# An LSTM's input term: added by TensorE from a ring of bfloat16 parts, or laid into PSUM by ScalarE

## The chip, the core and the metric

The kernel runs on one core of a Trainium2 chip. The metric is the device time of one execution in microseconds (us). Five engines work from queues of their own: TensorE (PE in the profile; PEld is its loading of weights), VectorE (DVE), ScalarE (ACT), GpSimd (POOL) and SyncE (SP), which only issues transfers here. They are ordered by semaphores alone: an instruction waits until a counter has reached a value and raises another when it is done. Before an engine stands a sequencer that reads the queue, does the register arithmetic and hands instructions on; its own instructions have the engine's name with a q in the profile (ACTq, DVEq).

## What is computed

The input x has 2 batches of 1024 time steps with 256 features. A first layer scales x by a conditioning vector, multiplies it by a weight, normalises it and adds it to x. The second layer, in which nearly all the time goes, is an LSTM over the 1024 steps, whose output is added to its input:

```python
xW = jnp.einsum('ntd,dk->tnk', x, Wx) + b
def step(carry, xw_t):
    prev_h, prev_c = carry
    a = xw_t + prev_h @ Wh
    i = jax.nn.sigmoid(a[:, :Hdim])
    f = jax.nn.sigmoid(a[:, Hdim:2 * Hdim])
    o = jax.nn.sigmoid(a[:, 2 * Hdim:3 * Hdim])
    g = jnp.tanh(a[:, 3 * Hdim:])
    next_c = f * prev_c + i * g
    next_h = o * jnp.tanh(next_c)
    return ((next_h, next_c), next_h)
```

Hdim is 256, so a step has 1024 gate values for each of the 2 batches, and each step needs the h of the one before.

## The kernel before

**Layout.** A feature lies on a partition: the 256 values of h are K = 2 chunks of 128 partitions, each with B = 2 batches, thus CB = 4 columns. The 1024 gate values are M = 8 chunks (two for each of the gates i, f, o, g), thus ITEMS = 16 columns of a step. x*Wx+b lies in the tile `xw` with the step as the fastest index (`xw[:, item, time in a block of 128]`). Only the first 17 items (chunk and batch of a block of 128 steps) are computed ahead of the loop (line 668); the loop computes one more in each of its turns and so keeps a block ahead.

**The loop** has 128 turns of 8 steps, written out; each engine has its own copy of it. In a step:

- TensorE (lines 505 to 559) does 12 matmuls that bring x*Wx+b into the gates' PSUM banks: `ring` holds it as three bfloat16 parts for 8 steps, and each part is multiplied by a bfloat16 identity (`input_apart`, `input_together`). They wait for `f_act`, `c_done` and `o_act`, that is, until ScalarE and VectorE have read what the last step left in the bank. In steps 2 to 7 of a turn it also does two of the 12 matmuls that project the item for a later block (`project`, 128 columns, bank X_BANK). Then it waits for `h_hi` and does 44 matmuls of Wh with h, both as two float16 parts, which accumulate onto the input: 8 for gate i with the high part of h, 8 for f (these wait for `h_lo`), 8 for g, 8 for i with the low part, 4 for half of o, 8 for the rest. After f, g, i and o they raise `f_mm`, `g_mm`, `ig_in`, `o0_mm` and `o_in`. All matmuls are recorded at line 389, the helper.
- VectorE (lines 697 to 726) sums the two halves of f (line 703) and of g (705), multiplies the cell state by sigmoid(f) (707), sums o (709), does the cell update as a scan (712), then the high part of h (715, raises `h_hi`), the low part (718, raises `h_lo`) and h itself for the output (722, raises `h_all`). In step 4 of a turn it also transposes the turn's output (726).
- ScalarE (lines 777 to 798) does the sigmoid of f (785), of i and g (788) and of o (790), and the tanh of the cell (792). In the last step of a turn it moves the projected item from PSUM into `xw` (797): it waits for `x_mm`, raises `act_seen` by a semaphore instruction, works out the addresses in registers, and does one ACTIVATE of 128 columns.
- GpSimd (lines 343 to 378) splits the next turn's x*Wx+b into three bfloat16 parts, four operations for each half of a turn (lines 287, 292, 297, 302), splits 8 steps of x in the same way (366 to 373), and adds the layer's input to h (308). Each group waits for a step's `h_all`.
- SyncE (from line 237) copies the weights and the piece of x for the next projection and stores the output.

**Ahead of the loop** VectorE works out scales (lines 629 to 646), which ScalarE needs to scale and split the weights (762 to 766, then GpSimd 319 and 322); TensorE projects the first 17 items and the first layer.

Of the kernel before, what the change touches and what calls it, by code (L numbers as in the profile page):

```python
# [27 lines left out]
P = 128  # L28
# [18 lines left out]
def cond_resid_lstm(nc, x, cond, w, wx, wh, bias, out):  # L47
# [13 lines left out]
    with ExitStack() as ctx:  # L61
# [13 lines left out]
        ident_b = sb("ident_b", [P, P], BF16)  # L75
# [15 lines left out]
        x_unit = sb("x_unit", [P, 1])  # L91
        w_scale = sb("w_scale", [P, 1])
# [3 lines left out]
        xw = sb("xw", [P, NI, P])  # L96
# [10 lines left out]
        ring = sb("ring", [P, UNROLL, G, 3, CB], BF16)  # L107
        rest = sb("rest", [P, M * B, HALF])
# [24 lines left out]
        pre_ig = psum[:, I_BANK:G_BANK + 1, sums]  # L133
        cell = banks[CELL][:, 0:3 * CB].rearrange("p (c s) -> p c s", s=3)
# [6 lines left out]
        s_zero, s_ident, s_identb, s_ones = sem("s_zero"), sem("s_ident"), sem("s_identb"), sem("s_ones")  # L141
# [12 lines left out]
        ring_full, ring_used = sem("ring_full"), sem("ring_used")  # L154
# [96 lines left out]
        def _(pool):  # L251
# [5 lines left out]
            pool.wait_ge(s_ident, 1)  # L257
            nc.gpsimd.tensor_copy(ident_b[:, :], ident[:, :]).then_inc(s_identb, 1)

            def xw_of_step(t0):

                block, inside = t0 // P, t0 % P
                if not isinstance(t0, int):
                    block, inside = pool.snap(block * ITEMS), pool.snap(inside)
                else:
                    block = block * ITEMS
                return xw[:, bass.ds(block, ITEMS), bass.ds(inside, HALF)]

            def parts(half, part):  # L270
                return ring[:, half * HALF:(half + 1) * HALF, :, part, :].rearrange("p s g c -> p g c s")

            def by_gate(ap):
                return ap.rearrange("p (g c) s -> p g c s", g=G)
# [5 lines left out]

            def xw_source(half, turn):

                return by_gate(xw_of_step(turn * UNROLL + half * HALF if isinstance(turn, int) else pool.snap(turn * UNROLL + half * HALF)))

            def split_high(half, src):

                nc.gpsimd.tensor_copy(parts(half, 0), src).then_inc(s_pool, 1)  # L287
                settle()

            def split_rest(half, src):  # L290

                nc.gpsimd.tensor_tensor(by_gate(rest[:, :, :]), src, parts(half, 0), ALU.subtract).then_inc(s_pool, 1)
                settle()

            def split_middle(half):

                nc.gpsimd.tensor_copy(parts(half, 1), by_gate(rest[:, :, :])).then_inc(s_pool, 1)  # L297
                settle()

            def split_low(half):  # L300

                nc.gpsimd.tensor_tensor(parts(half, 2), by_gate(rest[:, :, :]), parts(half, 1), ALU.subtract).then_inc(ring_full, 1)  # L302
# [21 lines left out]
            for s, v in last_read("xw"):  # L324
                pool.wait_ge(s, v)
            pool.wait_ge(s_start, 1)
            for half in range(2):
                src = xw_source(half, 0)
                split_high(half, src)
                split_rest(half, src)  # L330
                split_middle(half)
                split_low(half)
# [4 lines left out]
            def calm_after(step):  # L337

                pool.wait_ge(h_all, step)
                pool.sem_inc(pool_seen, 1)  # L340

            with pool.Fori(0, NI - 1) as i:
# [4 lines left out]
                pool.wait_ge(x_read, i + 1)  # L347
                pool.sem_inc(pool_seen, 1)
                for half in range(2):
                    done = t + (half + 1) * HALF  # L350
                    src = xw_source(half, i + 1)
                    pool.wait_ge(ring_used, 1)
                    pool.sem_inc(ring_used, -1)
                    calm_after(done)
                    split_high(half, src)
                    split_rest(half, src)
                    calm_after(done + 1)
                    if half == 0:
                        pool.wait_ge(y_turned, i + 1)
                        pool.sem_inc(pool_seen, 1)  # L360
                    save(half, t + half * HALF)
                    split_middle(half)
                    calm_after(done + 2)
                    split_low(half)
                    if half == 0:
                        nc.gpsimd.tensor_copy(part[0], now).then_inc(s_pool, 1)
                        settle()
                        calm_after(done + 3)
                        nc.gpsimd.tensor_tensor(res, now, part[0], ALU.subtract).then_inc(s_pool, 1)
                        settle()  # L370
                        nc.gpsimd.tensor_copy(part[1], res).then_inc(s_pool, 1)
                        settle()
                        nc.gpsimd.tensor_tensor(part[2], res, part[1], ALU.subtract).then_inc(x_split, 1)
# [7 lines left out]
        def _(pe):  # L381
# [98 lines left out]
            def in_ring(gate, u, part, first, last):  # L480
                return ring[:, u, gate, part, B * first:B * last].rearrange("p (c b) -> p c b", b=B)
# [343 lines left out]
```

## Time and profile of the kernel before

| | |
|---|---|
| median of 3 runs | 2023.9 us (2023.67 to 2024.75) |
| the profiled execution | 2023.3 us, of which its span (first to last instruction) is 2021.5 us |
| loop | 1024 steps, about 1.93 us each |
| busy share of the span | PE 98%, PEld 88%, DVE 63%, ACT 36%, POOL 30% |
| granted TensorE clock, mean | 0.51 of full speed |

A busy PE is not a PE at its peak: the matmuls are pipelined, and each is shown with its whole way through the array, 166 ns, while one starts about every 27 ns. The share therefore says little here; what waits for what in a step says more.

### The profile page before, as it was taken

What the parts mean: (1) busy time and instruction counts of PE and PEld (TensorE: products, weight loads), DVE (VectorE), ACT (ScalarE), POOL (GpSimd) and SP (SyncE); (2) the same over time, 40 slices, a digit from 0 to 9 for tenths busy, and PEclk for the clock granted to TensorE, in tenths of its full rate; (3) what the DMA queues carried; (4) which work ended last, traced back from release to release, by engine and by line L of the source; (5) the groups of instructions that cost most, each with busy time, mean ns of one, the idle gap of its engine ahead of it and who ended that gap; (6) DMA issues with size and microseconds to landing.
All of it is one profiled execution on the core that took longest, in us unless ns stands there. A gap on an engine that the chain in (4) does not pass through costs nothing.

```text
span 2021.5 us, 148186 instructions
## 1 busy us (share of the span) xinstructions
PE 1991.1 (98%) x59057; PEld 1770.8 (88%) x59057; DVE 1266.6 (63%) x8393; ACT 736.6 (36%) x4239; POOL 601.7 (30%) x1800
## 2 busy tenths in 40 slices
PE   8999999999999999999999999999999999999998
PEld 6888888888888888888888888888888888888887
DVE  6666666666666666666666666666666666666665
ACT  3333333333333333333333333333333333333333
POOL 2323233223323232332323233232323332332322
PEclk9555555555555555555555555555555555555555
DMA  2111111111111111111111111111111111111010
GB/s 96 21 21 27 20 21 26 21 20 21 27 20 21 23 24 20 21 27 20 20 21 26 20 21 27 21 20 21 27 20 21 23 24 20 21 27 20 21 22 20
DMA packets 188304, 48.63 MB, mean 24 GB/s; under 512 B 185468, under 2 KB 187784, under 8 KB 188296
## 3 DMA queue, kind: packets, MB, share of 16 engines
q1 hardware_dynamic: 188024, 48.26, 11.5%
q10 hardware_dynamic: 272, 0.26, 0.0%
q8 instruction: 5, 0.08, 0.0%
q14 instruction: 3, 0.02, 0.0%
HBM read 4.46 MB, written 2.10 MB: 3 GB/s over the span
## 4 chain that ended last, share of the span: by engine, by line
PE 95%; DVE 2%; ACT 1%; issue 1%; DMA 1%; SPq 0%; POOL 0%; POOLq 0%; DVEq 0%
PE psum L389 95%; DVE psum L712 1%; ACT scan_in L788 1%; DMA wx_sb<-in_L_cond_Wx_dram 1%; DVE psum L705 0%; DVE wmax L626 0%; SPq L203 0%; POOL wx_sb L315 0%; DVE xt L605 0%; SPq L205 0%; SPq L198 0%; SPq L199 0%; POOLq L61 0%; PE psum L435 0%; POOL y_cols L308 0%
## 5 line engine op out<-in xcount | busy, mean ns | idle before, releaser
L389 PE MATMUL psum<-h_parts,wh_p 128*128 128x2 f16 (+1 forms) x45056 | 1368.9, 166 | 0.0
L389 PEld LDWEIGHTS psum<-h_parts,wh_p 128*128 128x128 f16 x45056 | 1284.9, 104 | 46.8
L389 PE MATMUL psum<-ring,ident_b 128*128 128x4 bf16 (+2 forms) x12288 | 635.1, 168 | 19.1 <-DVE psum L680 2.6
L389 PEld LDWEIGHTS psum<-ring,ident_b 128*128 128x128 bf16 x12288 | 487.8, 105 | 185.0 <-DVE psum L712 165.0
L785 ACT ACTIVATE sig_f<-psum 128x4 f32<-128x4 f32 x1024 | 177.7, 174 | 1034.9 <-DVE psum L703 1034.9
L703 DVE TENSOR_REDUCE psum<-psum 128x4 f32<-128x8 f32 x1024 | 178.5, 174 | 389.0 <-PE psum L389 389.0
L389 PE MATMUL psum<-x_piece,wx_piece 128*128 128x128 bf16 x1536 | 411.0, 268 | 0.0
L715 DVE SCALAR_TENSOR_TENSOR h_parts<-scan_h 128x4 f16<-128x4 f32 x1024 | 174.2, 170 | 246.8 <-ACT scan_h L792 246.8
L287 POOL CAST ring<-xw 128x64 bf16 (+1 forms) x256 | 120.9, 472 | 601.0 <-DVE hring L722 600.8
L790 ACT ACTIVATE scan_h<-psum 128x4 f32<-128x4 f32 x1024 | 179.2, 175 | 142.3
L718 DVE TENSOR_TENSOR_SCAN h_parts<-scan_h,h_parts 128x12 f16<-128x12 f32 x1024 | 187.0, 183 | 35.0
L302 POOL TENSOR_TENSOR ring<-rest,ring 128x64 bf16<-128x64 f32 x256 | 124.8, 488 | 282.2 <-DVE hring L722 281.8
L705 DVE TENSOR_REDUCE psum<-psum 128x4 f32<-128x8 f32 x1024 | 178.5, 174 | 39.9
L788 ACT ACTIVATE scan_in<-psum 128x8 f32<-128x8 f32 x1024 | 185.4, 181 | 44.7
L712 DVE TENSOR_TENSOR_SCAN psum<-scan_in 128x12 f32<-128x12 f32 x1024 | 195.8, 191 | 0.0
L707 DVE TENSOR_TENSOR scan_in<-sig_f,psum 128x4 f32<-128x4 f32 x1024 | 164.3, 160 | 27.2
L792 ACT ACTIVATE scan_h<-psum 128x4 f32<-128x4 f32 x1024 | 179.8, 176 | 0.0
L709 DVE TENSOR_REDUCE psum<-psum 128x2 f32<-128x4 f32 x1024 | 174.4, 170 | 0.0
L389 PEld LDWEIGHTS psum<-x_piece,wx_piece 128*128 128x128 f16 x1536 | 159.8, 104 | 0.0
L722 DVE TENSOR_TENSOR hring<-scan_h 128x4 f32<-128x4 f32 x1024 | 153.6, 150 | 0.0
L297 POOL CAST ring<-rest 128x64 bf16<-128x64 f32 x256 | 120.7, 471 | 0.3 <-POOLq L279 0.3
L308 POOL TENSOR_TENSOR y_cols<-xt,hring 128x16 f32<-128x16 f32 x256 | 58.5, 229 | 208.5 <-DVE y_rows L726 115.7
(93 smaller groups left out, 410.4 us busy)
## 6 DMA issues: line engine op xcount, KB each, us to landing
x_piece<-x_p SPq DMA_DIRECT2D x128, 192.0 KB, 2.7
wx_piece<-wx_p SPq DMA_DIRECT2D x128, 128.0 KB, 2.4
out_dram<-y_rows SPq DMA_DIRECT2D x512, 4.0 KB
x_rows<-in_x_dram SPq DMA_DIRECT2D x4, 512.0 KB, 6.4
wh_sb<-in_L_cond_Wh_dram SPq DMA_DIRECT2D x1, 1024.0 KB, 9.7
wx_sb<-in_L_cond_Wx_dram SPq DMA_DIRECT2D x1, 1024.0 KB, 11.5
w_sb<-in_L_cond_weight_dram ACTq DMA_DIRECT2D x1, 256.0 KB, 2.8
small_rows<-in_cond_dram SPq DMA_DIRECT2D x1, 2.0 KB
```

The costliest lines, as they stand in the source:

```text
L389: return nc.tensor.matmul(out_, lhs, rhs, start=first, stop=last, skip_group_check=True)
L703: nc.vector.tensor_reduce(by_chunk(pre_f), parts_of(GATE_F, K), AX.X, ALU.add).then_inc(f_sum, 1)
L705: nc.vector.tensor_reduce(by_chunk(pre_g), parts_of(GATE_G, K), AX.X, ALU.add).then_inc(ig_in, 1)
L707: nc.vector.tensor_tensor(scan_b[:, :, 2], sig_f[:, :], cell[:, :, 2], ALU.mult).then_inc(cell_in, 1)
L709: nc.vector.tensor_reduce(by_chunk(pre_o0), parts_of(GATE_O, 1), AX.X, ALU.add).then_inc(o_in, 1)
L712: nc.vector.tensor_tensor_scan(flat(cell), flat(scan_a), flat(scan_b), 0.0, ALU.mult, ALU.add).then_inc(c_done, 1)
L715: nc.vector.scalar_tensor_tensor(out=h_parts[:, 0, :, 2], in0=scan_h[:, :, 1], scalar=2.0 ** H_SCALE, in1=scan_h[:, :, 2], op0=ALU.mult, o ...
L718: nc.vector.tensor_tensor_scan(flat(h_parts[:, 1, :, :]), flat(scan_h[:, :, :]), flat(h_parts[:, 0, :, :]), 0.0, ALU.mult, ALU.subtract).t ...
L785: nc.scalar.activation(sig_f[:, :], pre_f, ACT.Sigmoid, scale=unscale).then_inc(f_act, 1)
L788: nc.scalar.activation(sig_ig, pre_ig, ACT.Sigmoid, scale=unscale).then_inc(cell_in, 1)
L790: nc.scalar.activation(scan_h[:, :, 1].rearrange("p (h b) -> p h b", b=B), pre_o, ACT.Sigmoid, scale=unscale).then_inc(o_act, 1)
L792: nc.scalar.activation(scan_h[:, :, 2], cell[:, :, 2], ACT.Tanh).then_inc(t_done, 1)
```

## The change

ScalarE lays x*Wx+b of the next step into the gates' banks with five ACTIVATEs (function Copy) from `xw`, whose layout is turned so that the 16 columns of one step lie side by side. Where two columns of a bank are summed later (f, g and half of o), half of the value goes into each (`share` is 1 or 0.5). `h_hi` now counts three events a step: the copies of f and i, and the high part of h. The copies of g and o have semaphores of their own, for which TensorE waits in the midst of its 44 matmuls. `ring`, the bfloat16 split on GpSimd, the identity matmuls and their waits go.

```diff
-        xw = sb("xw", [P, NI, P])
+        xw = sb("xw", [P, T + UNROLL, ITEMS])
...
-        ring = sb("ring", [P, UNROLL, G, 3, CB], BF16)
-        rest = sb("rest", [P, M * B, HALF])
+        units = sb("units", [P, M])
```

GpSimd, in the loop (`after_step` is the old `calm_after`; the waits on `x_read`, `ring_used` and the four splitting operations of each half are gone):

```diff
+                after_step(t + 1)
+                nc.gpsimd.tensor_copy(part[0], now).then_inc(s_pool, 1)
+                settle()
+                after_step(t + 2)
+                nc.gpsimd.tensor_tensor(res, now, part[0], ALU.subtract).then_inc(s_pool, 1)
+                settle()
+                after_step(t + 3)
+                nc.gpsimd.tensor_copy(part[1], res).then_inc(s_pool, 1)
+                settle()
+                after_step(t + HALF)
+                pool.wait_ge(y_turned, i + 1)
                 pool.sem_inc(pool_seen, 1)
...
+                save(0, t)
+                after_step(t + HALF + 1)
+                nc.gpsimd.tensor_tensor(part[2], res, part[1], ALU.subtract).then_inc(x_split, 1)
+                after_step(t + UNROLL)
+                save(1, t + HALF)
```

TensorE:

```diff
                 for u in range(UNROLL):
-                    if u % HALF == 0:
-                        pe.wait_ge(ring_full, 2 * i + u // HALF + 1)
                     if u == FIRST_PIECE:
                         pe.wait_ge(x_staged, 32 * i + 32)
                         pe.wait_ge(x_read, i + 1)
-                    pe.wait_ge(f_act, t + u + 1)
-                    input_apart(GATE_F, u, 0, K)
                     if u >= FIRST_PIECE:
                         project(done)
                         done += 1
-                    pe.wait_ge(c_done, t + u + 1)
-                    input_apart(GATE_G, u, 0, K)
-                    input_together(GATE_I, I_BANK, u, 0, K)
-                    pe.wait_ge(o_act, t + u + 1)
-                    input_apart(GATE_O, u, 0, 1)
-                    last = input_together(GATE_O, O_REST, u, 1, K)
-                    if u % HALF == HALF - 1:
-                        last.then_inc(ring_used, 1)
                     if u >= FIRST_PIECE:
                         last = project(done)
                         done += 1
                         if done == len(terms):
                             last.then_inc(x_mm, 1)
-                    pe.wait_ge(h_hi, t + u + 1)
+                    pe.wait_ge(h_hi, (t + u + 1) * 3)
                     products(GATE_I, I_BANK, 0, 0, K)
                     pe.wait_ge(h_lo, t + u + 1)
                     products_apart(GATE_F, 0, K).then_inc(f_mm, 1)
+                    pe.wait_ge(g_add, t + u + 1)
                     products_apart(GATE_G, 0, K).then_inc(g_mm, 1)
                     products(GATE_I, I_BANK, 1, 0, K).then_inc(ig_in, 1)
+                    pe.wait_ge(o_add, t + u + 1)
                     products_apart(GATE_O, 0, 1).then_inc(o0_mm, 1)
```

VectorE, ahead of the loop and in it:

```diff
+            link(nc.vector.memset(share[:, :], 1.0))
+            nc.vector.memset(share[:, GATE_F * K:GATE_F * K + K + 1], 0.5)
+            link(nc.vector.memset(share[:, GATE_G * K:M], 0.5))
...
-            nc.vector.tensor_scalar(bias_s[:, :], small[:, B * K:NSMALL], scales[:, 0:1], None, ALU.mult).then_inc(s_bias, 1)
-            nc.vector.tensor_tensor(x_unit[:, :], scales[:, 0:1], scales[:, 3:4], ALU.mult).then_inc(s_bias, 1)
+            nc.vector.scalar_tensor_tensor(out=bias_s[:, :], in0=small[:, B * K:NSMALL], scalar=scales[:, 0:1], in1=share[:, :],
+                                           op0=ALU.mult, op1=ALU.mult).then_inc(s_bias, 1)
+            nc.vector.tensor_scalar(top[:, :], share[:, :], scales[:, 0:1], None, ALU.mult).then_inc(s_bias, 1)
+            link(nc.vector.tensor_tensor(x_unit[:, :], scales[:, 0:1], scales[:, 3:4], ALU.mult))
+            nc.vector.tensor_scalar(units[:, :], share[:, :], x_unit[:, :], None, ALU.mult).then_inc(s_bias, 1)
...
+            nc.vector.memset(xw[:, T:T + UNROLL, :], 0.0)
...
-                nc.vector.tensor_scalar(xw[:, v, :], bank[:, 0:P], scales[:, 0:1], bias_s[:, m:m + 1], ALU.mult, ALU.add).then_inc(s_dve, 1)
+                nc.vector.tensor_scalar(xw[:, (v // ITEMS) * P:(v // ITEMS + 1) * P, v % ITEMS], bank[:, 0:P], top[:, m:m + 1], bias_s[:, m:m + 1], ALU.mult, ALU.add).then_inc(s_dve, 1)
...
-                    dve.wait_ge(h_hi, step)
+                    dve.wait_ge(h_hi, dve.snap((t + u + 2) * 3))
```

ScalarE. The four `add_` functions are new; they are also called once ahead of the loop, for step 0:

```diff
+            def addends_of(step):
+                return xw[:, bass.ds(step, 1), :].rearrange("p t (m b) -> p m (t b)", b=B)
+            def in_two(source, gate):
+                return source[:, gate * K:(gate + 1) * K, :].unsqueeze(2).broadcast_to([P, K, 2, B])
+            def add_f(source):
+                nc.scalar.activation(ahead_f, in_two(source, GATE_F), ACT.Copy).then_inc(h_hi, 1)
+            def add_i(source):
+                nc.scalar.activation(ahead_i.rearrange("p (c b) -> p c b", b=B), source[:, GATE_I * K:(GATE_I + 1) * K, :], ACT.Copy).then_inc(h_hi, 1)
+            def add_g(source):
+                nc.scalar.activation(ahead_g, in_two(source, GATE_G), ACT.Copy).then_inc(g_add, 1)
+            def add_o(source):
+                first = GATE_O * K
+                nc.scalar.activation(ahead_o[0], source[:, first, :].unsqueeze(1).broadcast_to([P, 2, B]), ACT.Copy)
+                nc.scalar.activation(ahead_o[1], source[:, first + 1, :], ACT.Copy).then_inc(o_add, 1)
...
             with act.Fori(0, NI) as i:
                 t = i * UNROLL
-                item = act.snap((i + LEAD) % NI)
-                chunk = act.snap((item // B) % M)
                 for u in range(UNROLL):
                     step = act.snap(t + u + 2)
                     both = act.snap((t + u + 1) * 2)
+                    now = act.snap(t + u + 1)
                     act.wait_ge(f_sum, step)
                     nc.scalar.activation(sig_f[:, :], pre_f, ACT.Sigmoid, scale=unscale).then_inc(f_act, 1)
                     act.wait_ge(ig_in, both)
                     nc.scalar.activation(sig_ig, pre_ig, ACT.Sigmoid, scale=unscale).then_inc(cell_in, 1)
+                    if u == UNROLL - 1:
+                        act.wait_ge(x_read, i + 1)
+                    source = addends_of(now)
+                    add_f(source)
                     act.wait_ge(o_in, both)
                     nc.scalar.activation(scan_h[:, :, 1].rearrange("p (h b) -> p h b", b=B), pre_o, ACT.Sigmoid, scale=unscale).then_inc(o_act, 1)
                     act.wait_ge(c_done, step)
                     nc.scalar.activation(scan_h[:, :, 2], cell[:, :, 2], ACT.Tanh).then_inc(t_done, 1)
+                    add_i(source)
+                    add_g(source)
+                    act.wait_ge(o_act, step)
+                    add_o(source)
                     if u == UNROLL - 1:
+                        item = act.snap((i + LEAD) % NI)
+                        slot = act.snap(item % ITEMS)
+                        chunk = act.snap(slot // B)
+                        steps = act.snap((item // ITEMS) * P)
                         act.wait_ge(x_mm, i + 1)
                         act.sem_inc(act_seen, 1)
-                        nc.scalar.activation(xw[:, bass.ds(item, 1), :].rearrange("p n t -> p (n t)"), banks[X_BANK][:, 0:P], ACT.Identity,
-                                             bias=bias_s[:, bass.ds(chunk, 1)], scale=x_unit[:, :]).then_inc(x_read, 1)
+                        nc.scalar.activation(xw[:, bass.ds(steps, P), bass.ds(slot, 1)].rearrange("p t n -> p (n t)"), banks[X_BANK][:, 0:P], ACT.Identity,
+                                             bias=bias_s[:, bass.ds(chunk, 1)], scale=units[:, bass.ds(chunk, 1)]).then_inc(x_read, 1)
```

## Rows read from the trace of the kernel before

**Rows 1.** The page: busy time of each engine, and the chain that ended last

```profile
PE 1991.1 (98%) x59057; PEld 1770.8 (88%) x59057; DVE 1266.6 (63%) x8393; ACT 736.6 (36%) x4239; POOL 601.7 (30%) x1800
PE 95%; DVE 2%; ACT 1%; issue 1%; DMA 1%; SPq 0%; POOL 0%; POOLq 0%; DVEq 0%
```

**Rows 2.** The timeline of one step, 1002.6 to 1004.7 us: start, us busy, engine, line

```profile
1002.65 0.17 DVE L715 SCALAR_TENSOR_TENSOR h_parts<-scan_h 128x4 f16<-128x4 f32 x1 [0.24 <-ACT scan_h L792]
1002.75 0.27 PE L389 MATMUL psum<-x_piece,wx_piece 128*128 128x128 bf16 x1
1002.85 0.18 DVE L718 TENSOR_TENSOR_SCAN h_parts<-scan_h,h_parts 128x12 f16<-128x12 f32 x1
1002.87 1.25 PEld L389 LDWEIGHTS psum<-h_parts,wh_p 128*128 128x128 f16 x44
...
1003.71 0.17 ACT L785 ACTIVATE sig_f<-psum 128x4 f32<-128x4 f32 x1 [1.10 <-DVE psum L703]
1003.72 0.17 DVE L705 TENSOR_REDUCE psum<-psum 128x4 f32<-128x8 f32 x1
1003.92 0.16 DVE L707 TENSOR_TENSOR scan_in<-sig_f,psum 128x4 f32<-128x4 f32 x1
1003.93 0.18 ACT L788 ACTIVATE scan_in<-psum 128x8 f32<-128x8 f32 x1
...
1004.14 0.19 DVE L712 TENSOR_TENSOR_SCAN psum<-scan_in 128x12 f32<-128x12 f32 x1
1004.25 0.17 ACT L790 ACTIVATE scan_h<-psum 128x4 f32<-128x4 f32 x1
1004.37 0.18 ACT L792 ACTIVATE scan_h<-psum 128x4 f32<-128x4 f32 x1
...
1004.57 0.17 DVE L715 SCALAR_TENSOR_TENSOR h_parts<-scan_h 128x4 f16<-128x4 f32 x1 [0.24 <-ACT scan_h L792]
```

**Rows 3.** Groups of instructions, shapes kept apart: the parts that the change removes

```profile
L389 PEld LDWEIGHTS psum<-ring,ident_b 128*128 128x128 bf16 x12288 | 487.8, 105 | 185.0 <-DVE psum L712 165.0 <-issue 3.4
L302 POOL TENSOR_TENSOR ring<-rest,ring 128x64 bf16<-128x64 f32 x256 | 124.8, 488 | 282.2 <-DVE hring L722 281.8 <-POOLq L279 0.4
```

**Rows 4.** The timeline about a turn's end: line 715 ends steps 7 and 0

```profile
1014.21 0.17 DVE L715 SCALAR_TENSOR_TENSOR h_parts<-scan_h 128x4 f16<-128x4 f32 x1 [0.24 <-ACT scan_h L792]
1016.14 0.17 DVE L715 SCALAR_TENSOR_TENSOR h_parts<-scan_h 128x4 f16<-128x4 f32 x1 [0.24 <-ACT scan_h L792]
```

**Rows 5.** The same stretch on ScalarE alone, 1013.9 to 1015.3 us

```profile
1014.00 0.17 ACT L792 ACTIVATE scan_h<-psum 128x4 f32<-128x4 f32 x1
1014.48 0.46 ACT L797 ACTIVATE xw<-psum,bias_s,x_unit 128x128 f32 x1 [0.30 <-issue]
1015.27 0.17 ACT L785 ACTIVATE sig_f<-psum 128x4 f32<-128x4 f32 x1 [0.33 <-DVE psum L703]
```

**Rows 6.** ScalarE's sequencer there, by line: min/median/max ns, first and last start

```profile
L795 ACTq ALU_OP  x1: 38/38/38, 1014.0 to 1014.0; - x1
L796 ACTq EVENT_SEMAPHORE  x1: 17/17/17, 1014.1 to 1014.1; - x1
L797 ACTq FUSED_REGOPS  x2: 57/115/173, 1014.2 to 1014.4; - x2
L777 ACTq ALU_OP  x1: 35/35/35, 1014.5 to 1014.5; - x1
L777 ACTq COMPARE_BRANCH  x1: 45/45/45, 1014.6 to 1014.6; - x1
L777 ACTq FUSED_REGOPS  x1: 50/50/50, 1014.8 to 1014.8; - x1
```

**Rows 7.** Line 787's register operation, asked for 1013.34 to 1013.42 us

```profile
L787 ACTq ALU_OP  x1: 38/38/38, 1013.4 to 1013.4; - x1
```

**Rows 8.** Ahead of the loop: two ACTIVATEs in succession, and GpSimd's last split

```profile
33.77 0.20 ACT L752 ACTIVATE sig_f<-scales 128x1 f32<-128x1 f32 x1
33.88 0.19 ACT L753 ACTIVATE sig_f<-scales 128x1 f32<-128x1 f32 x1
32.89 4.07 POOL L322 TENSOR_TENSOR wx_p<-wx_s,wx_p 128x2048 f16<-128x2048 f32 x1
```

**Rows 9.** Ahead of the loop: the last scale on VectorE

```profile
24.53 0.15 DVE L646 TENSOR_TENSOR x_unit<-scales 128x1 f32<-128x1 f32 x1
```

**Rows 10.** Two stretches at the loop's start: busy PE, PEld, DVE, ACT, POOL, then PEclk

```profile
40.00:45.00 5.00, 2.23 (x68) 1.77 (x68) 2.32 (x10) 0.67 (x4) 1.22 (x3) 0.98 0.02 6
45.00:50.00 5.00, 5.00 (x159) 4.49 (x157) 3.05 (x21) 1.44 (x9) 0.00 (x0) 0.50 0.01 3
```

**Rows 11.** The loop's first matmuls with h, and the first and last high part of h

```profile
43.28 1.18 PEld L389 LDWEIGHTS psum<-h_parts,wh_p 128*128 128x128 f16 x44
44.94 0.17 DVE L715 SCALAR_TENSOR_TENSOR h_parts<-scan_h 128x4 f16<-128x4 f32 x1 [0.24 <-ACT scan_h L792]
...
2016.25 0.17 DVE L715 SCALAR_TENSOR_TENSOR h_parts<-scan_h 128x4 f16<-128x4 f32 x1 [0.24 <-ACT scan_h L792]
```

More of the change, by code:

```diff
@@ L91, in cond_resid_lstm @@
         x_unit = sb("x_unit", [P, 1])
+        share = sb("share", [P, M])
+        top = sb("top", [P, M])
         w_scale = sb("w_scale", [P, 1])
@@ L153, in cond_resid_lstm @@
         s_pool = sem("s_pool")
-        ring_full, ring_used = sem("ring_full"), sem("ring_used")
+        g_add, o_add = sem("g_add"), sem("o_add")
         hring_saved, pool_seen, store_seen = sem("hring_saved"), sem("pool_seen"), sem("store_seen")
@@ L256, in _ @@
                                     base=0, pattern=[[-1, P]], channel_multiplier=1).then_inc(s_ident, 1)
[L257 to L274, printed above, removed]
             def settle():
@@ L279, in settle @@
                 pool.sem_inc(s_pool, -1)
[L281 to L302, printed above, removed]
             def save(half, t0):
@@ L335, in _, with after_step @@
             res = x_rest[:, :, :, 0:UNROLL].rearrange("p k b t -> p (k b) t")
-            def calm_after(step):
+            def after_step(step):
                 pool.wait_ge(h_all, step)
@@ L475, in together @@
             def together(bank, first, last):
-                start = {I_BANK: 2 * CB, O_REST: 2 * CB - B}.get(bank, 0)
+                start = {I_BANK: 2 * CB, O_REST: 2 * CB - B}[bank]
                 return banks[bank][:, start + B * first:start + B * last].rearrange("p (c b) -> p c b", b=B)
-            def in_ring(gate, u, part, first, last):
-                return ring[:, u, gate, part, B * first:B * last].rearrange("p (c b) -> p c b", b=B)
-            def input_apart(gate, u, first, last):
-                columns = apart(gate, first, last)
-                mm(columns.rearrange("p c q b -> p q c b"), ident_b[:, :],
-                   ring[:, u, gate, 0:2, B * first:B * last].rearrange("p q (c b) -> p q c b", b=B), True, True)
-                return mm(columns[:, :, 0, :], ident_b[:, :], in_ring(gate, u, 2, first, last), False, True)
-            def input_together(gate, bank, u, first, last):
-                for part in range(3):
-                    mm_ = mm(together(bank, first, last), ident_b[:, :], in_ring(gate, u, part, first, last), part == 0, True)
-                return mm_
             def products(gate, bank, h_part, first, last):
@@ L678, in _ @@
                 dve.wait_ge(s, v)
-            nc.vector.memset(pre_f, 0.0).then_inc(h_lo, 1)
+            dve.sem_inc(h_lo, 1)
             nc.vector.memset(cell, 0.0).then_inc(c_done, 1)
@@ L775, in _ @@
             act.sem_inc(x_read, 1)
+            def addends_of(step):
[12 more added lines that the diff above has]
+                nc.scalar.activation(ahead_o[1], source[:, first + 1, :], ACT.Copy).then_inc(o_add, 1)
+            for s, v in last_read("xw") + last_read("x1"):
+                act.wait_ge(s, v)
+            act.wait_ge(s_start, 1)
+            for add in (add_f, add_i, add_g, add_o):
+                add(addends_of(0))
             with act.Fori(0, NI) as i:
                 t = i * UNROLL
-                item = act.snap((i + LEAD) % NI)
-                chunk = act.snap((item // B) % M)
                 for u in range(UNROLL):
```

54 lines of the change are left out of this document (11 added, 43 removed).

## The prediction, written before the changed kernel was run

> **What bounds the kernel now.** The page comes first: PE is busy 98% and is given 95% of the chain that ended last [rows 1]. That invites the wrong reading, because the change takes 12 of about 57 matmuls out of each step. So I read the timeline of one step [rows 2]. It is a ring of waits. Line 715 gives the high part of h at 1002.65; PE starts on h 0.22 later, at 1002.87, that is 0.05 after line 715's end. The 44 weight loads take 1.25, about 27 ns each. After 32 of them gates i and g are whole and line 788 starts at 1003.93, the cell scan (712) at 1004.14, the tanh (792) at 1004.37, the next line 715 at 1004.57. That is 1.92 us. The first and the last line 715 are 1971.31 us apart over 1023 steps, 1.927 each [rows 11]. Whatever is not in this ring costs nothing; the input matmuls stand between two bursts on h, while the scan, the tanh and line 715 run.
>
> The test for this is in the trace: steps 0 and 1 of a turn have no projection, steps 2 to 7 have two. Step 0 takes 1.93 from line 715 to line 715 [rows 4], no less than the step of [rows 2] with its projection. PE's backlog ahead of h delays nothing. It comes near: the last projection matmul starts at 1002.75, 0.12 before the matmuls on h [rows 2].
>
> Second, ScalarE's own queue. In a turn's last step line 797 starts 0.48 after the tanh, and the next step's first sigmoid (785) 1.27 after it [rows 5]. Between them lies register work of ScalarE's sequencer [rows 6]. When does it happen? Line 787's operation (38 ns) shows only from 1013.35 on, in an answer for 1013.34 to 1013.42 [rows 7]; the sequencer had nothing to do since the tanh at 1012.07, and line 785 started at 1013.34. So an instruction that waits holds up all behind it, register work too. That work is paid in line wherever instructions follow closely.
>
> **The change, part by part.**
>
> Removed from PE: 12288 matmuls, 487.8 us of weight loads [rows 3]. All lie ahead of `h_hi`, under the scan, tanh and line 715: 0. The projections and `x_mm` come some tenths earlier, and with them SP's two copies; they have over three steps until they are used: 0. The waits on `ring_full`, `f_act`, `c_done` and `o_act` go; h is still last.
>
> Removed from POOL: eight operations a turn (one group, 256 of 488 ns, in [rows 3]) with their waits. VectorE waits for POOL nowhere in the ring: 0. The order of what is left changes; each piece still has steps to spare.
>
> Added on PE: waits on `g_add` and `o_add` in mid-burst. Gate g's first matmul comes 16 loads, 0.43, after the start, gate o's 32 loads, 0.85. The copies will be done (below). A satisfied wait of this kind, `h_lo`, already stands in the burst, and 44 loads still take 1.25 [rows 2]: 0.
>
> Added on ScalarE in each step. No row shows an ACTIVATE from SBUF to PSUM whose address is in a register, so its place in the queue has to be bounded. Below: two in succession ahead of the loop start 0.11 apart [rows 8]. Above: no overlap, about 0.20 from start to start (0.175 of an ACTIVATE and a bit). Between: a register operation before each gives 0.02 + 0.038 + 0.07, where 0.07 is the gap from line 797's last register work to its start (asked for in 10 ns steps: it ends at 1014.415, [rows 5, 6]). I take 0.13, nearest to line 797, the one instruction with a register address.
>
> The copy of f stands between lines 788 and 790. Line 788 starts 0.32 before line 790 [rows 2]. The copy starts some 0.15 after 788, with 0.06 of register work, line 790 could go 0.11 later, at 0.26. It hides with 0.06 to spare: 0.
>
> The copy of i stands behind the tanh: it starts 0.13 later, takes 0.18, and has signalled by 0.35. PE waits for line 715's signal until 0.42. Line 718 on VectorE, which now waits for the copy as well, starts 0.40 after the tanh (0.20 behind line 715, which is 0.20 behind the tanh) [rows 2]. Hidden by 0.05: 0. The copies of g and o end by 0.31 + 0.39 = 0.70, against 0.42 + 0.43 and 0.42 + 0.85: 0.
>
> **ScalarE at the end of a turn** is another matter. Before, line 797's dispatch was at 0.48 after the tanh. Behind it come a register operation (35 ns), the branch (45) and the loop head's register work (50), the last from about 1014.79 to 1014.85 [rows 6]; with 0.07 more, line 785 could have started 0.44 behind line 797, at 0.92. It was due at 1.27. Slack: 0.35. Now four ACTIVATEs stand between the tanh and this tail: 4 x 0.13 = 0.52. And the address work grows: `item`, `slot`, `chunk`, `steps` and a second address for `units`. The six operations of 173 ns have three divisions or remainders in them, the three of 57 ns none [rows 6]; one more division and four or five simple ones make 0.08. So line 785 of a turn's step 0 comes 0.52 + 0.08 - 0.35 = 0.25 late. It drags lines 707, 788 and 712 along, because those were 0.21, 0.22 and 0.43 behind it with nothing between [rows 2]. PE's burst is over by then and cannot make up for it. 127 turn ends x 0.25 = 32 us. Bounds: 4 x 0.11 and no further address work give 0.09 late, 11 us; 4 x 0.20 and 0.17 (a second block of six) give 0.62 late, 79 us.
>
> The Trainium skill, "ScalarE: Activation LUTs", What ACT_TABLE_LOAD costs, says that back-to-back ACTIVATEs overlap by about 93 ns. By that alone four of 175 ns would take 0.33, the first sigmoid would come 0.06 late, and the sum would be 8 us; the pair of [rows 8], 0.20 long and 0.11 apart, agrees with the overlap, but had no register work between.
>
> Ahead of the loop: VectorE has a longer line for `bias_s`, `top`, a settled `x_unit` and `units`, some three operations of 0.15 [rows 9] with a wait, so 0.45; ScalarE's scaling starts behind it and GpSimd's last split (its end at 36.96, [rows 8]) with it. The loop's first 12 input matmuls go, about 0.3. GpSimd's first eight ring operations and the copies for step 0 are under other work. Bounds -0.3 to +0.5; I take 0.
>
> **Sum.** 2023.3 us of the profiled execution + 32 = 2055.3. The median of the runs is 0.6 above that execution, so against it the forecast is 2056.
>
> **Rivals.**
>
> No change. If ScalarE's sequencer does go ahead of a waiting instruction, or the tail's work is shorter than I think by 0.25, line 785 is in time and nothing is left: 2022 to 2026. For it: only 0.25 in 1.27 has to be wrong, the low bound is 0.09, and the rest of the step is hidden by my own count. Against: [rows 7]. It decides from 0.35 of added work in the tail. The Trainium skill, "Advanced Engine Details and Errata", Sequencer Loop and Engine Queue Depths, has the sequencer push an instruction into a queue of 8, where it waits for its semaphore while others are read; by that rule the register work would be done long before and the time be 2024. The trace disagrees: line 787's 38 ns come after line 785's start, not in the 1.2 us before it.
>
> Every step slower. The copy of f pushes line 790, and through it the tanh, which now start 0.12 apart. If the copy takes more than 0.21 of the 0.32, each 0.01 beyond costs 10 us. At 0.1 beyond (the 0.20 of the upper bound plus address work of 0.06) it is 0.04 to 0.1: 2056 + 41 to 100, so 2097 to 2160. Likewise the copy of i, if it signals after 0.42. Against: both have slack by the nearest rows.
>
> Faster. The ring shortens by PE's clock or by its free queue. The clock: the loop's first burst of 44 loads took 1.18 instead of 1.25 [rows 11], and the granted clock was 0.98 up to 45 us and 0.50 after [rows 10], the higher level of 2.4 GHz and then 1.2. At the higher one 32 loads save 0.05, 1024 x 0.05 = 52 us: 2004 with the tail's loss. Against: PE gets less to do, not more, and fell to the lower level with all 57 matmuls in a step. The queue: line 715 to PE would have to become shorter than 0.22; step 0 without projections has the same 1.93 [rows 4]. If only the tail were hidden as well, 1972.
>
> **How the numbers follow.** Late first sigmoid, 0.60, with its own range 2030 to 2090; no change 0.18; every step slower 0.13; faster 0.09. A measurement of this kernel can tell about 0.2%, 4 us, from no change. The late sigmoid at its low bound (11 us) is still beyond that. So slower 0.73, same 0.18, faster 0.09. The range reaches down over the no-change case to 2021 and up to 2090, which leaves out the faster case and most of every-step-slower.
>
> **What would show it.** Right: in the changed profile, line 797's successor starts 1.0 to 1.1 after the last step's tanh instead of 0.48, line 785 of step 0 about 1.5 after it instead of 1.27, in one step of eight; the other seven still take 1.92; ScalarE's busy time grows by about 5 x 1024 x 0.18 = 0.9 ms; POOL falls to a quarter or so; the granted clock stays near 0.5. Wrong: seven of eight steps longer or shorter than 1.92, a gap in the burst ahead of gate g or o, line 718 waiting for ScalarE, or a granted clock well above 0.5.

## The result and the profile of the changed kernel

| | before | changed |
|---|---|---|
| median | 2023.79 us (4 runs) | 2044.24 us (2043.6 to 2045.48, 4 runs) |
| ratio | | 1.01, 95% interval 1.0088 to 1.0112 |
| span of the profiled execution | 2021.5 us | 2041.7 us |
| granted TensorE clock, mean | 0.51 | 0.51 |

The change makes the kernel 20.5 us slower, 1.0%. The page shows what it did to the engines, beside [rows 1]:

```profile
PE 1584.1 (78%) x46769; PEld 1351.8 (66%) x46769; DVE 1264.0 (62%) x8398; ACT 1296.9 (64%) x9364; POOL 184.2 (9%) x775
PE 45%; ACT 28%; issue 12%; DVE 9%; ACTq 3%
```

TensorE lost 407 us of busy time, GpSimd 417, and the kernel is slower: what they lost was not in the ring of waits. ScalarE gained 560 us. On the chain that ended last, ACT now has 28%, and its sequencer, ACTq, has appeared with 3%. PE's share of that chain fell from 95% to 45%, although seven of eight steps take what they took before (below).

The timeline of ScalarE (start, us busy, engine, line) for the last two steps of a turn and the first of the next, with one line of VectorE, the sum of f (630, the old 703). Line 739 is the old 785 (sigmoid of f), 742 the old 788, 748 the old 790, 750 the tanh, 763 the old 797; 713, 716, 719, 723 and 724 are the copies:

```profile
1021.63 0.18 ACT L750 ACTIVATE scan_h<-psum 128x4 f32<-128x4 f32 x1
...
1022.90 0.17 ACT L739 ACTIVATE sig_f<-psum 128x4 f32<-128x4 f32 x1 [0.66 <-DVE psum L630]
...
1023.12 0.18 ACT L742 ACTIVATE scan_in<-psum 128x8 f32<-128x8 f32 x1
1023.31 0.18 ACT L713 ACTIVATE psum<-xw 128x8 f32 x1
1023.43 0.17 ACT L748 ACTIVATE scan_h<-psum 128x4 f32<-128x4 f32 x1
1023.55 0.17 ACT L750 ACTIVATE scan_h<-psum 128x4 f32<-128x4 f32 x1
1023.65 0.18 ACT L716 ACTIVATE psum<-xw 128x4 f32 x1
...
1024.00 0.17 ACT L724 ACTIVATE psum<-xw 128x2 f32 x1
...
1024.61 0.56 ACT L763 ACTIVATE xw<-psum,bias_s,units 128x128 f32 x1 [0.44 <-issue]
1024.62 0.17 DVE L630 TENSOR_REDUCE psum<-psum 128x4 f32<-128x8 f32 x1 [0.41 <-PE psum L334]
...
1025.02 0.17 ACT L739 ACTIVATE sig_f<-psum 128x4 f32<-128x4 f32 x1
1025.13 0.18 ACT L742 ACTIVATE scan_in<-psum 128x8 f32<-128x8 f32 x1
...
1025.64 0.18 ACT L750 ACTIVATE scan_h<-psum 128x4 f32<-128x4 f32 x1
```

From tanh to tanh the ordinary step takes 1.92 (1021.63 to 1023.55), as before. Over the turn's end it takes 2.09 (to 1025.64). There the sigmoid of f comes 1.47 behind the tanh, in the step before 1.27. Its wait on VectorE is gone from the row: line 630 started at 1024.62 and its sum was there by 1024.79, 0.23 before the sigmoid started. The excess of 0.165 us in 127 turn ends is 21 us.

The sequencer's work between the last copy and the next sigmoid, by line (min/median/max ns, first and last start), answers to [rows 6]:

```profile
L762 ACTq EVENT_SEMAPHORE  x1: 17/17/17, 1024.0 to 1024.0; - x1
L763 ACTq FUSED_REGOPS  x2: 176/179/182, 1024.1 to 1024.3; - x2
L763 ACTq ALU_OP  x1: 35/35/35, 1024.5 to 1024.5; - x1
L732 ACTq ALU_OP  x1: 35/35/35, 1024.6 to 1024.6; - x1
L732 ACTq COMPARE_BRANCH  x1: 45/45/45, 1024.7 to 1024.7; - x1
L732 ACTq FUSED_REGOPS  x1: 50/50/50, 1024.9 to 1024.9; - x1
```

The address work grew from 173 + 57 to about 358 + 35 ns. With line 795's operation of 38 ns, which stood behind the tanh before and has no counterpart there now, the growth is from 268 to 393 ns, 0.125 us. The loop head's register work ends by 1024.97, asked for in steps of 10 ns, and line 739 starts 0.05 behind it.

Ahead of the loop the first high part of h came at 44.42 instead of 44.94 [rows 11]:

```profile
44.42 0.17 DVE L642 SCALAR_TENSOR_TENSOR h_parts<-scan_h 128x4 f16<-128x4 f32 x1 [0.24 <-ACT scan_h L750]
...
2036.45 0.17 DVE L642 SCALAR_TENSOR_TENSOR h_parts<-scan_h 128x4 f16<-128x4 f32 x1 [0.24 <-ACT scan_h L750]
```

1992.03 us over 1023 steps is 1.9473 a step, 20.7 us more than before over the loop; less the 0.5 at the start, that is the 20.2 by which the spans differ. The 0.5 cannot be put down to the change: the kernels of experiments 1, 3 and 2 below have the same instructions ahead of the loop, and there the first high part of h came at 44.87, 44.97 and 46.79.

### The profile page after: what moved, and what is told of

The parts are those of the page before. It is cut to its first block, busy times and chain, and to the rows that moved or that the text cites. A ratio compares the mean times of both kernels' runs of the same rounds, so it can differ in the third digit from the quotient of the medians.

```text
span 2041.7 us, 131821 instructions
## 1 busy us (share of the span) xinstructions
PE 1584.1 (78%) x46769; PEld 1351.8 (66%) x46769; DVE 1264.0 (62%) x8398; ACT 1296.9 (64%) x9364; POOL 184.2 (9%) x775
## 4 chain that ended last, share of the span: by engine, by line
PE 45%; ACT 28%; issue 12%; DVE 9%; ACTq 3%
PE psum L334 45%; ACT scan_h L748 8%; DVE h_parts L642 8%; ACT psum L713 8%; ACT scan_h L750 6%; ACT scan_in L742 3%; ACTq L763 2%; ACT sig_f L739 1%; DVE psum L636 1%; ACTq L732 1%; ACT psum L719 0%; ACT psum L716 0%; DVE scan_in L634 0%; ACT psum L723 0%; ACTq L713 0%
## 5 line engine op out<-in xcount | busy, mean ns | idle before, releaser
L334 PE MATMUL psum<-x_piece,wx_piece 128*128 128x128 bf16 x1536 | 287.2, 291 | 0.0
L713 ACT ACTIVATE psum<-xw 128x8 f32 (+1 forms) x1025 | 184.7, 180 | 9.1 <-DVE xt L527 7.4
L719 ACT ACTIVATE psum<-xw 128x8 f32 (+1 forms) x1025 | 184.6, 180 | 0.0
L723 ACT ACTIVATE psum<-xw 128x4 f32 (+1 forms) x1025 | 181.5, 177 | 0.0
L716 ACT ACTIVATE psum<-xw 128x4 f32 (+1 forms) x1025 | 181.5, 177 | 0.0
L724 ACT ACTIVATE psum<-xw 128x2 f32 (+1 forms) x1025 | 174.3, 170 | 0.0
L763 ACT ACTIVATE xw<-psum,bias_s,units 128x128 f32 x128 | 72.3, 565 | 56.3 <-issue 56.3
```

The lines of the kernel that those rows point to most:

```text
L334: return nc.tensor.matmul(out_, lhs, rhs, start=first, stop=last, skip_group_check=True)
L713: nc.scalar.activation(ahead_f, in_two(source, GATE_F), ACT.Copy).then_inc(h_hi, 1)
L716: nc.scalar.activation(ahead_i.rearrange("p (c b) -> p c b", b=B), source[:, GATE_I * K:(GATE_I + 1) * K, :], ACT.Copy).then_inc(h_hi, 1)
L719: nc.scalar.activation(ahead_g, in_two(source, GATE_G), ACT.Copy).then_inc(g_add, 1)
```

## The experiments

The kernel before was run on the same chip beside each experiment, and its median lay between 2023.8 and 2025.7 us. So I compare ratios to it, not bare times; the changed kernel's own is 1.0101. `...` in a code cut stands for lines left out.

**1. The address work earlier.** Most of the register operations are done with explicit registers at the head of step 7, where ScalarE waits for the sum of f. The address in `xw` is also put together otherwise (one offset instead of two), so besides the place the split into blocks changes.

```diff
+                    if u == UNROLL - 1:
+                        act.reg_alu(place_r, act.snap(i + LEAD), NI, ALU.python_mod)
+                        act.reg_alu(slot_r, place_r, ITEMS, ALU.python_mod)
+                        act.reg_alu(chunk_r, slot_r, B, ALU.python_divide)
+                        act.reg_alu(place_r, place_r, ITEMS, ALU.python_divide)
+                        act.reg_alu(place_r, place_r, P * ITEMS, ALU.mult)
+                        act.reg_alu(place_r, place_r, slot_r, ALU.add)
                     act.wait_ge(f_sum, step)
...
-                        item = act.snap((i + LEAD) % NI)
-                        slot = act.snap(item % ITEMS)
-                        chunk = act.snap(slot // B)
-                        steps = act.snap((item // ITEMS) * P)
+                        chunk = act.snap(chunk_r, min_val=0, max_val=M - 1)
+                        place = act.snap(place_r, min_val=0, max_val=(T - P) * ITEMS + ITEMS - 1)
```

> The changed kernel with the address arithmetic of the turn's last ACTIVATE (item, slot, chunk, place in xw) moved from behind the copies of g and o to the head of step 7, where ScalarE waits for the sum of f anyway; same results. Theory (the tail of ScalarE's queue at the turn's end costs the 20 us): of the 0.47 us of register work between the last copy and that ACTIVATE about 0.3 goes, the first sigmoid of step 0 comes at its due time again (1.27 us after the tanh instead of 1.47), all eight steps take 1.925 us, time 2023 to 2025 us. Rival 1 (the ACTIVATE's own 565 ns or the four copies in front hold the sigmoid up, whatever the register work): at least 10 us of the 20 stay, 2034 or more. Rival 2 (the loss lies in every step): 2044, unchanged.

Measured: 2028.16 us beside 2025.33, ratio 1.0012 (1.0003 to 1.0021). ScalarE's timeline at a turn's end:

```profile
1013.81 0.18 ACT L758 ACTIVATE scan_h<-psum 128x4 f32<-128x4 f32 x1
...
1014.25 0.17 ACT L725 ACTIVATE psum<-xw 128x2 f32 x1
1014.55 0.56 ACT L769 ACTIVATE xw<-psum,bias_s,units 128x128 f32 x1
1015.08 0.17 ACT L747 ACTIVATE sig_f<-psum 128x4 f32<-128x4 f32 x1
```

Its address work there is two blocks, of 38 and 74 ns, instead of 393 ns; two blocks of 216 and 47 ns now stand at the head of step 7. So the sequencer has nearly as much to do, 375 ns, but only 112 of them in the tail. The ACTIVATE takes the same 565 ns, and all four copies are in front:

```profile
L740 ACTq FUSED_REGOPS  x1: 216/216/216, 1012.3 to 1012.3; - x1
L745 ACTq FUSED_REGOPS  x1: 47/47/47, 1012.6 to 1012.6; - x1
...
L765 ACTq FUSED_REGOPS  x1: 38/38/38, 1014.3 to 1014.3; - x1
L769 ACTq FUSED_REGOPS  x1: 74/74/74, 1014.4 to 1014.4; - x1
L769 ACT ACTIVATE xw<-psum,bias_s,units x1: 565/565/565, 1014.5 to 1014.5; 128x128 f32 x1
```

Line 769 starts 0.74 behind the tanh instead of 1.06, the sigmoid is back at 1.27, and the loss is gone but for 0.1%. The trace is of one of the shorter executions (2023.2 us, span 2021.3; the twelve took 2023.1 to 2030.9) and does not show where that 0.1% lies. This shows the mechanism: the queue's tail at the turn's end, and in it the sequencer's work. It leaves nothing for a loss in every step.

**2 and 3. One ACTIVATE more, in the tail or elsewhere** (the second kernel has `u < UNROLL - 1`).

```diff
                     add_o(source)
+                    if u == UNROLL - 1:
+                        nc.scalar.activation(spare[:, :], source[:, 0:K, :], ACT.Copy)
```

> The changed kernel with one ACTIVATE more (4 columns from xw to a spare tile) behind the copies of step 7, ahead of the address work. Theory (the queue of the turn's end is on the path): the next sigmoid comes 0.11 us later in 127 turns, 2044 + 14 = 2058 us. Rival (the last ACTIVATE waits for something else, such as PE's projection): 2044, unchanged.

> The changed kernel with the same one ACTIVATE more in steps 0 to 6 of each turn instead, seven times as many. Theory (ScalarE is idle 0.66 us there): nothing, 2042 to 2046 us. Rival (each ACTIVATE that is added costs its place in the queue, 0.11 us): 896 x 0.11 = 99 us, 2143.

Measured: 1.0122 (1.0108 to 1.0137) in the tail, 1.0097 (1.0082 to 1.0111) elsewhere, although that kernel has seven times as many. The two intervals overlap a little, but all four times of the first (2047.6 to 2052.2 us) lie above all four of the second (2043.3 to 2045.6). The place decides, as expected. The size was off: 0.2% or 4 us, not 14. The trace of the first has the reason:

```profile
1012.68 0.17 ACT L751 ACTIVATE scan_h<-psum 128x4 f32<-128x4 f32 x1
...
1013.23 0.19 ACT L757 ACTIVATE spare<-xw 128x4 f32 x1
1013.77 0.57 ACT L766 ACTIVATE xw<-psum,bias_s,units 128x128 f32 x1 [0.35 <-issue]
1014.18 0.17 ACT L740 ACTIVATE sig_f<-psum 128x4 f32<-128x4 f32 x1
```

The extra ACTIVATE starts 0.11 behind its neighbour, but line 766 starts 1.09 behind the tanh against 1.06 without it, and the sigmoid 1.50 against 1.47. The sequencer had gone on before the ACTIVATE began (its semaphore instruction shows at 1013.17, the ACTIVATE at 1013.23). In 127 turn ends 0.03 is 3.8 us. So an ACTIVATE that waited for no semaphore, and whose address was in a register already, cost the sequencer some 0.03 here. The four copies, 0.11 apart, each have a register operation of 43 to 46 ns of their own ahead of them; 0.11 is the place of such a pair, not of an ACTIVATE alone.

**4. A contiguous write.**

```diff
+            nc.gpsimd.memset(xw[:, P:T, :], 0.0).then_inc(s_clean, 1)
...
-                        nc.scalar.activation(xw[:, bass.ds(steps, P), bass.ds(slot, 1)].rearrange("p t n -> p (n t)"), banks[X_BANK][:, 0:P], ACT.Identity,
+                        nc.scalar.activation(aside[:, :], banks[X_BANK][:, 0:P], ACT.Identity,
```

> The changed kernel with the turn's last ACTIVATE writing its 128 columns side by side into a tile of their own instead of every 16th column of xw; GpSimd zeroes xw ahead of the loop. It leaves out x*Wx+b from step 129 on, so the outputs are not the layer's. Theory: the 565 ns (457 before the change) come from the stride of the write, so the ACTIVATE is back at about 457; the next sigmoid follows 0.41 us behind it as now, because the sequencer's branch and loop head set that; the address of the write also goes, about 6 operations, 0.1 to 0.2 us less of register work, so 2024 to 2036 us. Rival (the second address in a register, for scale, makes the 565): the duration stays at 565.

Measured: the ACTIVATE takes 457 to 459 ns with the register address for `units` still in it, so the stride of 64 bytes, not this second register address, makes 565. One block of register work (180 ns) and one operation (35 ns) are left; line 766 starts 0.85 behind the tanh, the sigmoid at its due 1.27. The ratio of 1.0043 holds a later start: line 766 first shows at 66.9 us, its counterpart in the changed kernel at 58.8, since GpSimd's zeroing takes 12 us ahead of the loop and VectorE waits for it. This experiment takes out a block of address work together with the stride, so it settles the 565 ns, and by itself not which of the two brings the sigmoid back; experiment 1 does, where the 565 ns stayed.

**5. Twelve matmuls back on TensorE.**

```diff
+                    for _ in range(12):
+                        mm(banks[UNUSED][:, 0:4], wh_p[:, 0, 0, 0:P], wh_p[:, 1, 0, 0:4], True, True)
                     pe.wait_ge(h_hi, (t + u + 1) * 3)
```

> The changed kernel with 12 matmuls of 4 columns again in each step ahead of the wait for h, into an unused bank and without waits: TensorE has as much to do as before. Theory (these matmuls were hidden, so taking them out saved nothing): 2042 to 2046 us. Rival (taking them out did save, and ScalarE's copies cost more than the 20 us that show): slower, by 12 x 27 ns x 1024 = 330 us at the most.

Measured: ratio 1.0108 (1.0093 to 1.0122), which holds the changed kernel's 1.0101. In the traces a step takes 1.950 us in the mean against 1.947, 3 us over the loop. So what the change took off TensorE was worth nothing that the ratios can tell, and 0.15% by the traces.

**6. Two ACTIVATEs more ahead of the sigmoid of o**, in each step: the price of the rival "every step slower".

```diff
                     add_f(source)
+                    nc.scalar.activation(spare[:, 0, :], source[:, 0:K, :], ACT.Copy)
+                    nc.scalar.activation(spare[:, 1, :], source[:, 0:K, :], ACT.Copy)
                     act.wait_ge(o_in, both)
```

> The changed kernel with two ACTIVATEs of 4 columns more between the copy of f and the sigmoid of o in each step. It prices the rival that the copy of f displaces the path in every step. The copy starts 0.12 behind the sigmoid of i and g, the sigmoid of o is due 0.33 behind it. If each takes its place of 0.11: the sigmoid of o comes at 0.46 instead of 0.33 and the tanh with it, 1024 x 0.13 = 133 us, 2177 us. If only the sequencer's 0.05 count: 0.12 + 0.11 + 0.1 = 0.33, 2044 to 2060 us.

Measured: 2083.05 us, ratio 1.0296 (1.0279 to 1.0313), between the two: 1.95% over the changed kernel, 0.04 a step. In an ordinary step:

```profile
1014.92 0.18 ACT L743 ACTIVATE scan_in<-psum 128x8 f32<-128x8 f32 x1
...
1015.36 0.15 ACT L751 ACTIVATE scan_h<-psum 128x4 f32<-128x4 f32 x1
1015.41 0.17 ACT L753 ACTIVATE scan_h<-psum 128x4 f32<-128x4 f32 x1
```

The sigmoid of o comes 0.44 behind line 743 instead of 0.33, close to the 0.46 of the first branch. But the tanh follows it by 0.05, not by 0.12: in the changed kernel the tanh started when the cell was there (line 639, 1023.33 + 0.19, the tanh at 1023.55), and 0.07 of the 0.12 absorbs the delay. So the single copy of f in the change had more room than I had counted.

**7. Does TensorE's clock decide?** Six kernels, all with the early addresses of experiment 1. First one matmul into the unused bank in each step's pause, of 256 or 512 columns (512 shown):

```diff
+                    mm(banks[UNUSED][:, 0:512], wh_p[:, 0, 0, 0:P], wh_p[:, 1, 0, 0:512], True, True)
                     pe.wait_ge(h_hi, (t + u + 1) * 3)
```

> The kernel with the early addresses (2028 us beside 2025 before) plus one matmul of 256 columns in each step ahead of the wait for h, into an unused bank. It is a test of the rival that TensorE's clock decides. If more columns in the idle time bring the granted clock to the higher level, 32 weight loads take 0.05 us less and the step 1.875: 1975 us. Theory: the clock stays at 0.51 and the filler, 0.21 us, is hidden by the 0.36 to 0.6 us that TensorE is idle: 2024 to 2030 us.

> The same with 512 columns in each step. If the granted clock goes to the higher level, 1975 us. If it stays low, the filler takes 0.43 us; steps 0 and 1 (idle 0.6) hide it, steps 2 to 7 (idle 0.36) are 0.05 to 0.1 longer: 768 x 0.07 = 54 us, 2080 us.

Measured: ratios 1.0007 (0.9998 to 1.0017) and 1.0007 (0.9997 to 1.0016), granted clock 0.51 in both. The 512 columns did not lengthen the steps, against my 54 us: in the pause TensorE had room for them.

Then the 44 matmuls themselves eight times as wide: the h columns repeated by a stride of 0, the copies into columns of the bank that nothing reads; alone, and with one matmul of 512. One of the two helpers is shown, the other is changed alike:

```diff
-                            mm_ = mm(together(bank, c, c + 1)[:, 0, :], wh_p[:, w_part, k, m * P:(m + 1) * P],
-                                     h_parts[:, h_part, k * B:(k + 1) * B, 2], False, True)
+                            mm_ = mm(banks[bank][:, col:col + 16 * 8].rearrange("p (r x) -> p r x", x=16)[:, :, 0:B], wh_p[:, w_part, k, m * P:(m + 1) * P],
+                                     h_parts[:, h_part, k * B:(k + 1) * B, 2].unsqueeze(1).broadcast_to([P, 8, B]), False, True)
```

> The kernel with the early addresses, and each of the 44 matmuls moves 16 or 32 columns instead of 2 or 4: the same columns of h eight times, the copies into unused columns of the bank. At 1.2 GHz 32 columns take 27 ns, what a weight load takes anyway. It asks again whether a busier TensorE gets the higher clock. If it does: 32 loads at 25 instead of 26.7 ns save 0.05 us a step, the longer matmuls cost 0.01, time 2025 - 40 = 1985 us. Theory (the clock stays at 0.51): the last columns of a matmul come 28 / 1.2 = 23 ns later and the results with them, 2025 + 24 = 2049 us.

> The same with one matmul of 512 columns in each step's pause as well, so that TensorE's array moves columns nearly all the time. If the higher clock comes, 1985 us. If not, as without the filler or a little more, 2049 us.

Measured: alone 1.0092 (1.0068 to 1.0117) at a clock of 0.51, with steps of 1.947 us instead of 1.927, the 20 us of longer matmuls; with the filler 0.9943 (0.9911 to 0.9976) at a mean clock of 0.821, between the two times expected. Stretches of the second (busy PE, PEld, DVE, ACT, POOL, then the granted clock):

```profile
1000.00:1004.00 4.00, 4.00 (x105) 2.94 (x102) 2.36 (x16) 2.41 (x18) 0.45 (x2) 0.50 0.05 12
1008.00:1012.00 4.00, 3.45 (x109) 2.79 (x105) 2.44 (x17) 2.44 (x18) 0.47 (x2) 1.00 0.02 3
1016.00:1020.00 4.00, 4.00 (x104) 2.94 (x102) 2.46 (x17) 2.52 (x19) 0.45 (x2) 0.50 0.00 0
```

The clock goes between 1.2 and 2.4 GHz within one execution; steps take 1.95 at the lower level and 1.90 at the higher. So next come two matmuls of 512 in the pause, three in steps 0 and 1; and last the same filler with the 44 matmuls narrow again:

```diff
+                    for _ in range(2 if u >= FIRST_PIECE else 3):
+                        mm(banks[UNUSED][:, 0:512], wh_p[:, 0, 0, 0:P], wh_p[:, 1, 0, 0:512], True, True)
```

> The kernel with the early addresses, the 44 matmuls eight times as wide, and in each step's pause two matmuls of 512 columns (three in steps 0 and 1, which have no projection). With one of 512 the granted clock went up and down, 0.82 in the mean; steps at the higher clock took 1.90 us, those at the lower 1.95. If more columns keep it at the higher level, all steps take 1.90: 1024 x 1.90 + 52 around the loop = 1998 us, faster than both kernels by over 1%. If it still falls now and then, the steps at the lower clock are longer by up to 0.5 us, since 1024 to 1536 columns take 0.85 to 1.28 us there and TensorE's pause is 0.4 to 0.6: 2020 us or more.

> The kernel of 1998 us with the 44 matmuls back to 2 and 4 columns; the two or three matmuls of 512 columns in each pause stay. If the filler alone holds the higher clock, a step needs no longer the 0.02 us for the wide matmuls: 1024 x 1.88 + 52 = 1977 us. If the wide matmuls are needed as well, the clock stays at the lower level, where the 1024 to 1536 columns take 0.85 to 1.28 us of a pause of 0.4 to 0.6: steps longer by 0.4 to 0.5 us, 2450 us.

Measured: with the wide matmuls 1998.07 us beside 2024.63, ratio 0.9867 (0.9851 to 0.9883), clock 0.996; with the narrow ones 2399.58 us, ratio 1.1849 (1.1829 to 1.1869), clock 0.508. The first holds the higher level from 50 us on:

```profile
45.00:50.00 5.00, 5.00 (x98) 3.39 (x99) 2.21 (x15) 2.30 (x18) 0.21 (x1) 0.66 0.02 3
50.00:55.00 5.00, 4.89 (x143) 3.87 (x142) 2.97 (x22) 2.86 (x23) 0.45 (x2) 1.00 0.02 5
```

It computes the same outputs and beats both kernels, with steps of 1.90. In the narrow one, three matmuls of 512 start at 1001.10 and the next ones with h only at 1002.34, though line 644 gave h at 1001.60:

```profile
1001.10 1.44 PE L334 MATMUL psum<-wh_p 128*128 128x512 f16 x3
1001.60 0.17 DVE L644 SCALAR_TENSOR_TENSOR h_parts<-scan_h 128x4 f16<-128x4 f32 x1 [0.24 <-ACT scan_h L760]
1002.34 0.83 PE L334 MATMUL psum<-h_parts,wh_p 128*128 128x2 f16 x24
```

Which property of the matmuls brings the level is left open; these six kernels only show which of them had it.

## Why the prediction was right, point by point

- **The ring of waits, not PE's busy share, bounds the kernel.** Right. Ordinary steps stayed at 1.92, and twelve matmuls more or less move 0.15% by the traces and nothing clear of noise.
- **The sequencer does not go past an instruction that waits.** Right as far as it was used. The changed kernel repeats it: line 739 waits from 1022.24 to 1022.90, and the operation behind it, line 741's, shows only at 1022.9. ("Nothing to do since the tanh" was not exact: one operation, line 784's, came right behind the tanh; the pause behind it is as the prediction reads it.) Experiment 1 moves most of this register work from behind a run of ACTIVATEs into a wait, and 18 of the 20 us go. The queue that the Trainium skill describes ("Advanced Engine Details and Errata", Sequencer Loop) shows too, where the ACTIVATE waits for nothing: in experiment 2 the sequencer was ahead of the ACTIVATE by 0.06.
- **The tail's sum: 32 us, measured 20.** The mechanism held; four terms were mis-sized. "4 x 0.13 = 0.52": the copies start 0.11 apart and the last begins 0.45 behind the tanh. "0.08" of growth in address work: it is 0.13 (0.61 from the last copy to line 763, against 0.48 from the tanh before). These two nearly cancel, which is luck. That a block has six operations, or three, was read from the code; no row shows it. The turn's head was 0.41, not 0.44. Together line 739 is 0.20 late, not 0.25. And "with nothing between" was wrong by 0.035: behind a late sigmoid of f, line 742 follows by 0.11 rather than 0.22, since its own input is long there; the scan (639) then follows line 634 by 0.19 (1025.23, 1025.42) instead of 0.23 (1023.10, 1023.33), and only 0.165 reaches the tanh. 127 x 0.165 = 21 us. The forecast interval of this case, 2030 to 2090, holds 2044.
- **The copies of f and i hide.** Right. The copy of f starts 0.12 behind line 742 in an ordinary step and 0.19 in step 7, where the sigmoid of o is on time as well. Behind line 642, PE starts on h after 0.22 and line 645 after 0.20, both as before, so the copy of i delays neither.
- **Ahead of the loop: taken as 0**, bounds -0.3 to +0.5; it was -0.5 in this trace, outside them. Since the same instructions gave anything from 44.42 to 46.79 in other runs, the bounds were too near for one execution, and what the change does there is not shown.
- **The signs.** The ones about the tail came as written (line 763 1.06 behind the tanh, line 739 1.47). ScalarE's busy time grew by 0.56 ms, not 0.9: the prediction counted 0.18 for each of five ACTIVATEs, and they overlap, so that each adds its 0.11.
- **The rivals.** "No change" would have needed 0.2 less in the tail; experiment 1 is that case, made on purpose. "Every step slower" is refuted. Its price, 0.04 to 0.1 a step for 0.1 too much, held at its lower end in experiment 6 (0.04 for 0.11), but "each 0.01 beyond costs 10 us" did not: the first 0.07 costs nothing. "Faster" by the clock: right that this change does not bring it, and right in the price, 0.05 a step (1.95 against 1.90 in experiment 7); that more work would bring it was not foreseen, beyond saying that PE gets less to do.

## What to carry to other kernels

Ask of an engine off the path not only how busy it is but what stands in its queue right ahead of the next instruction that is due, register work and branch included, and look at the step where everything comes together, not at the mean one. A loop's address arithmetic belongs into a place where the engine waits anyway; here moving six written register operations (263 of 375 ns) was worth 0.9%. Work taken off an engine that the chain names at 95% saved nothing here, because it did not lie behind the wait that ends last.

## What I had not expected

Adding work to TensorE made the kernel faster: 1024 to 1536 columns in each pause, and seven of eight in each matmul with h, that nobody reads, gave 1.3% less time than the kernel before, through the granted clock. The clock of 0.51 had looked like a property of the kernel. The other surprise is the price of a stride: 128 columns written 64 bytes apart take 565 ns, side by side 457. And blocks of register work differ widely: those of the address work that the compiler makes from remainders and divisions take 173 to 198 ns, experiment 1's at the head of step 7 takes 216, while its last one ahead of line 769 takes 74 and the loop head's 50.
